# Silu on ScalarE as one instruction over all channel groups, in place of tanh, plus one and products

## The reference

```
xz = h @ in_w
xs, z = jnp.split(xz, 2, axis=-1)
xc = sum(conv_w[:, k] * xp[:, k:k + L, :] for k in range(4)) + conv_b
xc = jax.nn.silu(xc)
dbl = xc @ xproj_w                      # gives dt, B and C
delta = jax.nn.softplus(dt @ dt_w + dt_b)
h[t] = exp(delta * A) * h[t-1] + delta * B * xc
y = (sum over states of h * C + Dp * xc) * jax.nn.silu(z)
```

## Time and profile before

| | us |
|---|---|
| median of 3 runs (5057.02 to 5060.24) | 5058.52 |
| profiled execution | 5060.27 |
| its span, first to last instruction | 5058.5 |

### The profile page before, as it was taken

The page is one execution under the profiler, slowest core; times in us unless marked ns, Lnnn a source line. Parts: engine busy times, 40 slices in busy tenths (PEclk is TensorE's granted clock), DMA queues, the critical chain, the costliest instruction groups (busy, mean ns, idle before and its releaser), DMA issues. The chain is left out here.

```text
span 5058.5 us, 45264 instructions
## 1 busy us (share of the span) xinstructions
PE 4220.2 (83%) x13994; PEld 1806.9 (36%) x13994; DVE 3725.3 (74%) x4812; ACT 2358.3 (47%) x3535; POOL 2615.4 (52%) x2093
## 2 busy tenths in 40 slices
PE   5988888888889888888888988884398898889865
PEld 1333223233233223322223322331255555546543
DVE  4999899899899989989989998996402534424436
ACT  4565555565555555556555665553201222222214
POOL 3777787778777778767878777883000000000000
PEclk8999999999999999999999999997699998999976
DMA  2433444344344434434434443442301002010000
GB/s 86 131 121 116 129 128 128 113 128 130 117 132 120 121 125 128 125 116 127 130 117 130 122 125 117 131 126 58 95 7 39 16 16 52 4 30 4 16 1 13
DMA packets 136613, 463.87 MB, mean 92 GB/s; under 512 B 20847, under 2 KB 23346, under 8 KB 134494
## 3 DMA queue, kind: packets, MB, share of 16 engines
q1 hardware_dynamic: 136318, 460.42, 30.2%
HBM read 434.43 MB, written 21.43 MB: 90 GB/s over the span
## 5 line engine op out<-in xcount | busy, mean ns | idle before, releaser
L669 POOL TENSOR_TENSOR prod<-states,c_rows 128x512 f32<-128x512 f32 x1536 | 1954.4, 1280 | 703.5 <-DVE states L586 690.9
L586 DVE TENSOR_TENSOR_SCAN states<-decay,carry,bpsum 128x512 f32<-128x512 f32 x1536 | 1946.3, 1268 | 0.7 <-ACT decay L448 0.6
L342 PE MATMUL ypsum<-prod,identity 128*128 128x512 f32 x3072 | 1624.5, 612 | 4.0
L448 ACT ACTIVATE decay<-delta,decay_rate 128x512 f32<-128x512 f32 x1536 | 1079.0, 715 | 604.7 <-DVE states L586 553.6
L575 DVE TENSOR_TENSOR bpsum<-bpsum,dx 128x512 f32<-128x512 f32 x1536 | 1040.3, 678 | 117.0 <-PE bpsum L335 116.0
L335 PE MATMUL bpsum<-b_rows,select 96*128 96x512 bf16 x1536 | 614.8, 403 | 426.2 <-DVE states L586 380.0
L342 PEld LDWEIGHTS ypsum<-prod,identity 128*128 128x128 f32 x3072 | 599.7, 198 | 338.6 <-issue 191.8
L335 PEld LDWEIGHTS bpsum<-b_rows,select 96*128 96x128 bf16 x1536 | 150.1, 98 | 1388.2 <-DVE states L586 1040.3
L1077 PE MATMUL convp<-img_hi,w_hi 96*96 96x512 f16 (+1 forms) x1568 | 484.5, 386 | 58.6 <-PEq L1455 42.8
L1425 DVE SCALAR_TENSOR_TENSOR x<-convp,unscale,x_group 96x1024 f32<-96x1024 f32 x16 | 20.4, 1278 | 407.9 <-PE convp L1077 407.9
L1077 PE MATMUL convp<-img_hi,w_lo 128*96 128x512 f16 (+1 forms) x896 | 275.9, 387 | 0.0
(11 more groups left out here) (217 smaller groups left out, 4728.9 us busy)
## 6 DMA issues: line engine op xcount, KB each, us to landing
c_rows<-c_map SPq DMA_DIRECT2D x512, 512.0 KB, 3.7
c_rows<-c_map SPq DMA_DIRECT2D x512, 256.0 KB, 3.9
x_in<-in_x SPq DMA_DIRECT2D x18, 384.0 KB, 5.0
fused_map<-fused SPq DMA_DIRECT2D x17, 384.0 KB, 4.2
work<-fused_map SPq DMA_DIRECT2D x4, 1536.0 KB, 9.3
x<-in_x SPq DMA_DIRECT2D x4, 1536.0 KB, 15.5
x_biased_map<-work SPq DMA_DIRECT2D x4, 1536.0 KB, 7.1
x_group<-x_biased_map SPq DMA_DIRECT2D x16, 384.0 KB, 4.2
```

The lines of the kernel that those rows point to most:

```text
L342: pe.matmul(ypsum[:, group % Y_BANKS, :], identity[:, :], prod[:, n % P_RING, :], start=s == 0, stop=s == STATES - 1).then_inc(summed, 1)
L448: act.activation(decay[:, n % RING, :], delta[k % 2][:, g, :], ACT.Exp, scale=decay_rate[:, k // 2, g, s:s + 1]).then_inc(decay_ready, 1)
L586: dve.tensor_tensor_scan(states[:, n % H_RING, :], decay[:, n % RING, :], bpsum[:, n % B_BANKS, :], carry[:, k, u:u + 1], ALU.mult, ALU.ad ...
L669: pool.tensor_tensor(prod[:, n % P_RING, :], states[:, n % H_RING, :], c_rows[:, n // C_STATES % C_RING, n % C_STATES, :], ALU.mult).then_ ...
```

## The change

ACT computes silu itself with its Silu function: one instruction over all three groups for x, written to `xc`, in slot 26 behind the copy of group 2, and one for z, written to `gate`, in slot 31. The copies no longer halve, and the bias is no longer halved at setup. The tanh instructions, the plus one, DVE's three products and POOL's three products are gone. Behind each Silu the table with exp and ln is loaded again; the load of Silu's own table in front of it is put in by the compiler. The load ahead of softplus is gone. The projections wait once per step for all of `xc`, and DVE waits for the gate where it uses it.

```diff
-    "x01_copy": (21, 21, 2), "x2": (23, 23, 3), "x2_copy": (26, 26, 1), "tanh_x": (24, 24, 1),
-    "xc": (25, 25, 1), "tanh_x2": (26, 26, 1), "xc2": (27, 27, 1), "z2": (25, 25, 1),
+    "x01_copy": (21, 21, 2), "x2": (23, 23, 3), "x2_copy": (26, 26, 1), "silu_x": (26, 26, 1),
+    "z2": (25, 25, 1),
-    "tanh_z": (30, 30, 1), "gate": (31, 31, 2), "hi": (32, 32, 2), "rest": (33, 33, 1),
+    "silu_z": (31, 31, 1), "hi": (32, 32, 2), "rest": (33, 33, 1),
...
-                    dve.tensor_scalar(cols[:, :, :, 0:1], cols[:, :, :, 0:1], 0.5, None, ALU.mult)
...
-                            pe.wait_ge(xc_ready, 3 * q + g + 1)
+                            pe.wait_ge(xc_ready, q + 1)
...
-                            act.activation(xpre[:, g, :], mm[:, g % 2, :], ACT.Identity, scale=0.5,
+                            act.activation(xpre[:, g, :], mm[:, g % 2, :], ACT.Identity,
                                            bias=cols[:, layer, g, conv_b:conv_b + 1]).then_inc(bank_read[g % 2], 1)
...
-                            act.activation(zpre[:, g, :], mm[:, bank, :], ACT.Copy, scale=0.5).then_inc(bank_read[bank], 1)
-
-                        for i in due("tanh_x", layer, at, 1) + [1 for _ in due("tanh_x2", layer, at, 1)]:
-                            gs = (slice(0, 2), slice(2, 3))[i]
-                            for bank in range(2 if i == 0 else 1):
-                                use = pro_use(q, bank, X_FIRST if i == 0 else G2)
-                                act.wait_ge(bank_read[bank], use + 1)
-                            act.activation(tmp1[:, gs, :], xpre[:, gs, :], ACT.Tanh).then_inc(tanh_x, 1)
-                        for i in due("tanh_z", layer, at, 1):
+                            act.activation(zpre[:, g, :], mm[:, bank, :], ACT.Copy).then_inc(bank_read[bank], 1)
+
+                        for i in due("silu_x", layer, at, 1):
+                            act.wait_ge(bank_read[1], pro_use(q, 1, X_FIRST) + 1)
+                            act.wait_ge(bank_read[0], pro_use(q, 0, G2) + 1)
+                            act.activation(xc[pair][:, :, :], xpre[:, :, :], ACT.Silu).then_inc(xc_ready, 1)
+                            act.preload_act_table_set(LN_EXP_SET)
+                        for i in due("silu_z", layer, at, 1):
                             for bank in range(2):
                                 act.wait_ge(bank_read[bank], pro_use(q, bank, Z_FIRST) + 1)
-                            act.activation(tmp2[:, :, :], zpre[:, :, :], ACT.Tanh).then_inc(zpre_ready, 1)
-                            act.wait_ge(zpre_ready, q + 1)
-                            act.activation(tmp2[:, :, :], tmp2[:, :, :], ACT.Copy, bias=1.0).then_inc(tanh_z, 1)
+                            act.activation(gate[pair][:, :, :], zpre[:, :, :], ACT.Silu).then_inc(gate_ready, 1)
+                            act.preload_act_table_set(LN_EXP_SET)
...
-                                act.wait_ge(gate_ready, 3 * step if not only_prologue else 3)
+                                act.wait_ge(gate_ready, step if not only_prologue else 1)
...
-                            if g == 0:
-                                act.preload_act_table_set(LN_EXP_SET)
                             act.activation(tmp2[:, g, :], zpre[:, g, :], ACT.Ln).then_inc(log_ready, 1)
...
+                    def j_of(group):
+                        return group // GROUPS
+
...
+                            if j_of(group) > 0 and units:
+                                dve.wait_ge(gate_ready, j_of(group))
                             dve.tensor_tensor(yy[:, g, :], y, gate[pair][:, g, :], ALU.mult).then_inc(gated, 1)
...
-                        for g in due("xc", layer, at, 2) + [2 for _ in due("xc2", layer, at, 1)]:
-                            dve.wait_ge(tanh_x, 2 * q + g // 2 + 1)
-                            dve.scalar_tensor_tensor(xc[pair][:, g, :], tmp1[:, g, :], 1.0, xpre[:, g, :],
-                                                     ALU.add, ALU.mult).then_inc(xc_ready, 1)
...
-                        for g in due("gate", layer, at, GROUPS):
-                            pool.wait_ge(tanh_z, q + 1)
-                            pool.tensor_tensor(gate[pair][:, g, :], tmp2[:, g, :], zpre[:, g, :], ALU.mult).then_inc(gate_ready, 1)
```

## The result

The changed kernel takes 5095.59 us, median of 4 runs (5091.95 to 5106.19), where the kernel before took 5059.38 on the same chip (4 runs, 5057.02 to 5062.17). The ratio is 1.0075, with a 95% interval from 1.0057 to 1.0092: slower by three quarters of a per cent, as forecast, and 3.6 us above the predicted 5092. The profiled execution has a span of 5092.4 us, 33.9 more than before; the worked sum was 33.2. Its mean granted clock is 0.935 (before 0.936).

A forecast was written before the change was run, and what follows sets the result against it. PE was taken to bound slots 19 to 32, DVE the rest of each step; 32 x 0.96 = 30.7 us plus 2.5 made 33.2, so 5093.5 from the profiled 5060.27, forecast as 5092 us, range 5056 to 5125.

The forecast's parts named there:

- PE sets slots 19 to 32: Part of each step with projections between unit matmuls: PE paces it, busy 36.00 of 36.00 us, while DVE waits.
- DVE's three products and its waits: xc products dropped per step, 1.8 us, with 4.0 us of waits: gain nothing, reappearing as waits for PE's broadcast.
- POOL's three products: Gate products dropped per step, 124.1 us in all with 70.2 us of waits in front: gain nothing.
- the load of softplus: Table load dropped in the DVE-paced part: nothing gained in the loop, 1.28 us saved in the first step.
- Silu costs what tanh costs: On ACT, each Silu over 128x1536 taken at 1.47 us, as tanh, with 0 to 1 us more for the range.
- rival 4: Silu takes 1 us longer than Tanh: 2.3 us per step, 72 us, 5133 us; chance 0.07.
- The loads: ACT's table loads around both Silus: 1.28 us each, 132 in place of 66.
- rival 3: Each table switch costs 1.4 us of drain more: 5.7 us per step, 182 in all, about 5243 us; chance 0.03.
- The late copy of z2: ACT, slots 26 to 28: load, Silu, load delay this copy, so PE's second z matmul starts 0.96 us late per step.
- The Silu of z fits: ACT at slot 31: load, Silu, load end before dt_rows is due, slack 0.7 us, so it costs nothing.
- The first step: Serial step ahead of the loop: second z matmul 3.8 us late, less 1.28 for softplus's load, +2.5 us net.
- The sum: Loop's 32 x 0.96 = 30.7 us plus 2.5 for the step ahead of it: 33.2 us.

The follow-up runs named there:

- e9: e1 with the first of four convolution taps left out, 4 of 16 x matmuls per step: 4944.09 us, ratio 0.9769.
- e1: Changed kernel with Silu's table load at slot 26 issued before ACT waits for x2, not behind its copy: 5057.76 us, ratio 0.9994.
- e2: Changed kernel with Copy in place of Silu for x and both table loads of slot 26 gone: 5053.42 us, ratio 0.9985.
- e5: Changed kernel with one more table load, of another table, behind the Silu of x: 5185.67 us, ratio 1.0253.
- e3: Changed kernel with Copy in place of Silu for z and both table loads of slot 31 gone: 5095.1 us, ratio 1.0069.
- e4: Changed kernel with one more table load, of another table, behind the Silu of z: 5103.94 us, ratio 1.0083.

## Why the prediction was right

**PE sets slots 19 to 32: shown.** e9 takes work from PE and gains all of it; e1 has less work than the kernel before on DVE and POOL and gains nothing. The rule of the Trainium skill (Trainium Kernel Development and Optimization, section "Performance Expectations") that busy weight loads tell more than busy matmuls is about the distance from the peak; as a sign of which engine is the bound it would have led astray here: weight loads were busy 12.6 of 36 us, yet PE was the bound.

**DVE's three products and its waits, POOL's three products, the load of softplus, worth nothing: shown together,** not one by one, for the steady step (102.24 in e1 against 102.23); in all e1 is at 0.9994. They turned up as waits for the broadcast, but not by the full amount forecast: +161.8 us in e1 (277.8 against 116.0), where 191 was said; the +203.5 of the changed kernel has the stalls of PE in it. The difference of 29 us didn't reach the time and isn't followed further.

**Silu costs what tanh costs: right,** 1487 and 1483 ns against 1471 for tanh, so rival 4 is out. **The loads: right,** 132 of 1283 ns, and the Silu starts 0.01 us behind its load. That excludes rival 3. The Trainium skill (ScalarE: Activation LUTs, section "What ACT_TABLE_LOAD costs") adds 1.38 us of drain per switch; none of these loads shows it.

**The late copy of z2: right, a little small.** The copy came 5.49 us after that of x2 (5.41 worked out: the load starts 0.08 behind the copy, where I had taken 0.03, and the Silu is 0.02 longer). L405 starts 1.01 us late against 0.96; its pair then takes 1.13 instead of 1.02, which I had not thought of. So a step is 1.13 longer (102.23 to 103.36; the 102.6 and 103.6 of the prediction come from a step that isn't a steady one). e1 and e2 cure it at either load, e5 doubles it.

**The Silu of z fits: right,** slack 0.94 (0.7 said); e3 and e4 put a price on both sides of it.

**The first step: mis-sized.** Up to dt_rows +3.8 was worked out; the 1.28 of the load of softplus, which makes +2.5 of it, is saved only behind dt_rows (e1 shows it: 93.65 us to the next dt_rows in place of 94.93). dt_rows came at 77.56 where it came at 70.82, 6.7 later. Of this 0.5 was there when the z matmuls of two groups began: x_in came 1.06 later, and the x matmuls took 10.02 us in place of 10.59. PE's timeline of that step:

```profile
68.89 2.07 PE L405 MATMUL mm<-h_norm,w_z 96*128 96x512 f32 x2 [3.63 <-ACT zpre L496]
70.75 7.74 PE L413 MATMUL mm<-xc,w_proj 128*108 128x512 f32 x12
```

The wait is as forecast, 3.63 against 3.8. But the pair takes 2.07, where the pair ahead of the wait takes 1.13, and the twelve matmuls 7.74, which took 6.03 before. The window behind the idle time has a granted clock of 0.69, a mix of the two levels as in e5:

```profile
68.00:78.00 10.00, 9.11 (x14) 2.08 (x14) 0.00 (x0) 6.39 (x8) 0.00 (x0) 0.69 0.00 0
```

**The sum.** From the first dt_rows to the last the change adds 32.05 us, where 30.7 less 1.28 were said. It isn't 32 x 1.13 = 36.2, since the steps that cross into a trip grew less, by 6.0 us for all eight (889.5 to 895.5). With the first step's 6.7 that is 38.8. The span grew by 33.9: 4.9 us came back behind the last dt_rows, for the most part in the second phase, which the change doesn't touch, and as much lies within what this stretch varies by from run to run (1610 to 1620 us in all the runs here). So the mechanism and the size of a step were right, and that 33.2 met 33.9 to within a us is luck: two terms were too small and the noise took them back.

One slip in the part on the kernel before: z0 is copied in slot 28 and z1 in slot 29, z2 in 27. The times were read from the timeline, so no step hangs on it.

## What to carry to other kernels

A table load needs no data: issue it ahead of the wait for the data, in the idle time, and not behind it; here that single line is worth 38 us. Price an inserted instruction by which instruction of the engine that sets the stretch has to wait for what stands behind it, and not by busy shares, and don't count on work taken off an engine that waits. When such an engine waits, move the heavy stage into the slots where it is late, but keep the next deadline (here dx of the next step): two slots with softplus held back gave 39 us on e1 and 29 on the kernel before; with softplus moved as far they gave none.

## What the runs showed of the hardware

A stall of PE can have a second price. With 0.85 us of idle time (the changed kernel, all 32 steps of the loop) the granted clock stayed at 1.00 and only 0.11 us was lost behind it. With 2.13 to 2.14 us (e5) it fell in 25 of 32 steps; in the one shown it was 0.61 for the 3.4 us behind, and the steady step lost another 1.69 us, more than the added wait itself. In the first step of the changed kernel 3.63 us of idle time left 0.69 in the 10 us behind. Where between 0.85 and 2.14 us this begins, and why the stalls of the 7 steps that cross from one trip to the next escaped it, was not tried.

A table load took 1283 ns in every group, and the ACTIVATE behind it started 0.01 us after its end. Silu, Tanh and Copy over 128x1536 took 1483 to 1487, 1471 and 1483 ns.
